# Two up-products of the token-routed experts moved ahead of the output block of the first half's tiles

## The reference

```python
expert_ids = jnp.minimum(clip(token_ids, 0, 12499) // 3125, 3)
for e in range(4):
    g = silu(einsum('bsd,fd->bsf', x, W[e]))
    u = einsum('bsd,fd->bsf', x, W[e])
    y = einsum('bsf,df->bsd', g * u, W[e])
    out = where((expert_ids == e)[..., None], y, out)
x = layernorm(x + out)
```

## Time and profile before

| | |
|---|---|
| median of 3 runs | 702.3 us (701.1 to 705.02) |
| the profiled execution | 701.97 us |
| its span, first to last instruction | 699.9 us |
| TensorE busy | 659.2 us (94%) |
| VectorE busy | 468.1 us (67%) |
| ScalarE, GpSimd busy | 348.6 us, 346.6 us |
| mean granted TensorE clock | 0.990 of full |

### The profile page before, as it was taken

The page is one execution under the profiler, slowest core; times in us unless marked ns, Lnnn a source line. Parts: engine busy times, 40 slices in busy tenths (PEclk is TensorE's granted clock), DMA queues, the critical chain, the costliest instruction groups (busy, mean ns, idle before and its releaser), DMA issues.

```text
span 699.9 us, 12735 instructions
## 1 busy us (share of the span) xinstructions
PE 659.2 (94%) x4598; PEld 511.8 (73%) x4598; DVE 468.1 (67%) x1085; ACT 348.6 (50%) x807; POOL 346.6 (50%) x476
## 2 busy tenths in 40 slices
PE   8989989899999888889999999999999999999994
PEld 6856668857466645557888888887579888888884
DVE  6579878463154999998866867775375556666555
ACT  4655536151514746356877877776352222222224
POOL 5325416341102786555786766766424444455421
PEclk9999999999999999899999999999999999999998
DMA  8000007001003000000000100000202111111001
GB/s 284 1 2 3 1 2 300 1 1 50 0 1 85 2 15 1 2 1 0 2 1 1 70 1 2 1 1 2 68 23 68 46 46 46 46 45 46 1 1 60
DMA packets 10351, 23.31 MB, mean 33 GB/s; under 512 B 2033, under 2 KB 5074, under 8 KB 9906
## 3 DMA queue, kind: packets, MB, share of 16 engines
q1 hardware_dynamic: 10002, 22.24, 9.6%
q10 hardware_dynamic: 288, 0.26, 0.1%
HBM read 21.45 MB, written 1.05 MB: 32 GB/s over the span
## 4 chain that ended last, share of the span: by engine, by line
PE 75%; DVE 16%; ACT 4%; issue 2%; POOL 1%; DMA 1%; POOLq 0%; SPq 0%; DVEq 0%; ACTq 0%
PE psum L454 42%; DVE A L1504 6%; PE psum L1090 4%; PE psum L1101 4%; PE psum L515 4%; PE psum L492 4%; PE psum L859 2%; PE psum L568 2%; PE psum L910 2%; PE psum L610 1%; DVE A L1368 1%; DVE stats L1241 1%; PE psum L574 1%; DVE x_tok L1238 1%; PE psum L584 1%
## 5 line engine op out<-in xcount | busy, mean ns | idle before, releaser
L454 PE MATMUL psum<-parts 128*128 128x256 f32 (+2 forms) x1440 | 244.1, 327 | 2.2 <-DVE C L1540 1.1
L454 PEld LDWEIGHTS psum<-parts 128*128 128x128 f32 (+1 forms) x1440 | 213.8, 190 | 30.3 <-issue 3.3
L2137 POOL TENSOR_SCALAR probs<-probs,row_rec 128x256 f32<-128x256 f32 x128 | 70.2, 561 | 47.3 <-DVE row_rec L1312 44.3
L2051 ACT ACTIVATE A<-psum 128x512 f32<-128x512 f32 x44 | 26.3, 598 | 115.6 <-PE psum L454 115.5
L1733 ACT ACTIVATE probs<-probs,neg_max 128x256 f32<-128x256 f32 x128 | 63.8, 500 | 32.8 <-DVE neg_max L1303 32.8
L1504 DVE TENSOR_TENSOR_SCAN A<-decay,psum 128x256 f32<-128x256 f32 x128 | 75.4, 663 | 4.2 <-PE psum L910 4.2
L1623 DVE TENSOR_TENSOR A<-A,psum 128x512 f32<-128x512 f32 x44 | 30.1, 686 | 70.6 <-ACT A L2051 58.4
L1303 DVE CUSTOM_DVE_ANT_0 probs<-psum,ctxT 128x256 f32<-128x256 f32 x128 | 48.9, 419 | 38.8 <-PE psum L454 36.7
L454 PE MATMUL psum<-parts,A_rounded 128*128 128x256 f32 x372 | 56.2, 289 | 2.4 <-DVE A_rounded L1444 2.4
L454 PEld LDWEIGHTS psum<-parts,A_rounded 128*128 128x128 f32 x372 | 50.1, 196 | 3.7 <-DVE A_rounded L1444 2.8
L1661 DVE TENSOR_TENSOR parts<-A,parts 128x512 fp32r<-128x512 f32 x44 | 48.9, 1111 | 0.8 <-ACT parts L2058 0.7
(11 more groups left out here) (257 smaller groups left out, 1261.7 us busy)
## 6 DMA issues: line engine op xcount, KB each, us to landing
A<-in_experts SPq DMA_DIRECT2D x12, 384.0 KB, 3.1
C<-in_experts SPq DMA_DIRECT2D x10, 384.0 KB, 3.0
A<-in_w_o SPq DMA_DIRECT2D x1, 2048.0 KB, 12.6
x_tok<-in_x_tok SPq DMA_DIRECT2D x1, 1024.0 KB, 7.1
ctxT<-in_ctxT SPq DMA_DIRECT2D x1, 1024.0 KB, 10.5
A<-in_w_uqT SPq DMA_DIRECT2D x1, 768.0 KB, 6.2
out<-x_tok SPq DMA_DIRECT2D x6, 128.0 KB, 1.8
xT<-in_xT SPq DMA_DIRECT2D x2, 256.0 KB, 4.0
```

The lines of the kernel that those rows point to most:

```text
L454: ins = mm(o, left[l], right[r], start=first and n == 0, stop=last and n == 2, skip_group_check=True)
L2137: last = pool.tensor_scalar(pr, pr, row_rec[:, u % RING[n], j:j + 1], 1.0, ALU.mult, ALU.mult)
```

## The change

TensorE issues the up-products 12 and 13 ahead of the output block of the first half's tiles instead of behind it. No other engine's program changes.

```diff
             up_high(1)
             up_low(0)
             up_low(1)
-            for k in range(2, 12):
+            for k in range(2, 14):
                 if k == 4:
                     ln_transposes(0, 1)
                 up(k)
             final(1, range(4), out1)
-            for k in range(12, 16):
+            for k in range(14, 16):
                 if k == 15:
                     ln_transposes(1, 0)
                 up(k)
```

## The result

The changed kernel took 704.64 us in the median (703.44 to 709.21, 20 runs) against 702.4 (700.71 to 708.46, 20 runs) for the kernel before: ratio 1.0032, 95% interval 1.0017 to 1.0047. It is slower by 2.2 us. That is less than the 0.5% (3.5 us) which the forecast took as the least that can be told, but the interval is clear of one. The forecast was 702.7 in a range of 700.7 to 704.8, and no difference.

The account below looks back on a forecast made before the run. TensorE, busy 94% of the span, was taken as the bound, with VectorE setting the pace just ahead of the block. Late start + 0.4, clock - 1.4 and + 1.7 gave + 0.7 on 701.97: 702.7 us, range 700.7 to 704.8.

Parts of the forecast that it names:

- The late start of the block: First half's output block: product 13 waits for VectorE's product 9, so the block starts 0.41 us late (0.2 to 0.6).
- The idle that moves: Ahead of the normalised tokens' transposes: TensorE idles about 2.8 us, transposes stay 4.17 us behind the block, 2.75 us saved worth nothing.
- The rival in which it isn't needed: Ahead of the transposes: tokens ready earlier, so transposes start when product 14 ends; 698.1 us, chance 0.04.
- The clock: Half-clock falls: the one at 125.75 us in the block goes (1.42 us gained), one behind the new idle comes (1.7 lost).
- the idle moves and the fall moves with it: Main case: fall at the block goes, one comes behind the new idle at the transposes; 702.7 us, chance 0.46.
- the slower rival: The fall in the output block stays and another comes behind the new idle; + 2.1 us, 704.1 us, chance 0.12.

Follow-up runs that it names:

- The two fillers: Unused extra matmuls in TensorE's long idle: ten ahead of the transposes in the changed kernel, mean 702.67 us; nine ahead of the block in the kernel before, 701.88 us.

## Why the prediction was right, and what it got wrong

The forecast of no difference held because 2.2 us is below what it took as tellable. The number was less good: the forecast was 0.7 us above the profiled execution, or 0.3 above the median, and the changed kernel is 2.2 above. 704.64 lies 0.16 us inside the upper end of the range, which had been drawn for a rival whose mechanism didn't happen. That the value falls inside is partly luck.

**The late start of the block** was forecast at 0.41 us. Counted from VectorE's product 8, the block starts 126.82 - 122.96 = 3.86 us behind it instead of 3.27: 0.59 us. Product 12 and product 13 each started 0.15 us after VectorE's product had ended (123.63 to 123.78, 125.21 to 125.36) and not 0.06, and each took 1.46 to 1.58 us from start to start, not 1.37. Behind the block's start 0.1 us comes back: 18.36 us to the hidden products in the changed kernel's fourth trace (126.50 to 144.86), 18.49 in the second of before (125.84 to 144.33), both at full clock. So 0.46 us remain, near the forecast and inside its bounds of 0.2 to 0.6.

**The idle that moves** was right: 2.8 us forecast, 2.76 to 2.78 in four traces; the transposes stayed 4.15 us behind the block. That a cover there is worth nothing beyond the tokens' arrival is shown best by three products moved. The rival in which it isn't needed is out.

**The clock** is the term that was mis-sized. I took one fall away ahead of the block (1.42 us) and put one behind it (1.7), as if both kernels had exactly one in each execution: + 0.3 net. Each price was about right: 1.41 us for the block, and behind the new idle 1.1 (19.49 against 18.38), 1.2 (149.13 - 129.55 = 19.58 in the third trace) and 1.6 (in the second, 19.31 - 18.36 up to the hidden products and 7.70 - 7.03 in them). How often was not: the changed kernel spends 3.8 +- 0.6 us more per execution at half clock. At 0.35 us for each that is 1.3 us. With the 0.46 it makes 1.8 of the 2.18 +- 0.28 us between the means, and 0.4 is left. Taken execution by execution, with 0.35 us off for each us at half clock, the changed kernel stays 0.82 +- 0.18 us above the kernel before, where the late start gives 0.46; whether that is noise or a term that nobody named isn't shown. The two fillers size the clock without the slope: filling the idle took 2.31 +- 0.35 us off the changed kernel's mean and 0.92 +- 0.49 off that of the kernel before, so the new idle costs 1.4 +- 0.6 us more than the old one, not 0.3. The step that failed is "the idle moves and the fall moves with it": the longer idle costs more clock than the shorter one, on the mean, and falls elsewhere may be part of it. The value of 704.1 that I gave for the slower rival was nearer to the measured one, but its mechanism (the fall in the block stays) is not what happened: the block took 11.68 us in all four traces of the changed kernel.

**What stays open.** Filling the new idle took away 6.0 +- 0.7 us at half clock, more than one fall of 3.4 us, and no trace shows two behind that idle. So part of the clock's cost lies in falls elsewhere, and no run shows how the idle brings them. In the changed kernel 3 of 4 traces had a fall near 220 us and in the kernel before none of 3, but 4 of the 7 others had one too. Whether the change makes that fall likelier, or the four traces were unlucky, these runs don't settle. That the difference of the first two traces lay mostly there is therefore no proof that the change caused it. The gain of the kernel with one product moved, 0.34 +- 0.40 us in the mean, is also not shown. No version beat the kernel before by more than its interval.

## What to carry to other kernels

Work that is moved into an idle of its engine must not be the cover of another wait: what counts is the next point where that engine meets the others, and here both meetings hang on VectorE. If work has to be moved, split it so that both idles stay short, though a gain in time by this isn't shown here: one product moved leaves 0.8 and 1.4 us with no fall behind either in two traces, two leave 2.8 us in one piece. A fall costs only where TensorE sets the pace: look up how far apart two rows around it are in a trace with it and in one without. Where times differ by less than a fall or two of the clock, count the time at half clock over many executions, not the falls of two traces.

## What the runs showed of the hardware

A fall of the same length has very different prices by place: 3.4 us at half clock cost 1.41 us in the block of 96 matmuls, 1.1 to 1.6 us behind the new idle, 1.6 us near 220 us (19.83 against 18.22 us) and nothing near 258 us, where TensorE had to wait for VectorE's L1504 four times between 255 and 259 us in the changed kernel's first trace.

A matmul that waits for VectorE's semaphore started 0.15 us after the end of VectorE's instruction in the changed kernel, both for product 12 and product 13, against 0.06 us at the block in the kernel before.

Every fall in the body lasted 3.4 us or twice that, and its place against the same idle varied: at 142.1, with the idle still on, or at 143.5, 1.4 us after its end. In the latter case (second trace of the changed kernel) it reached into the hidden products, which then took 7.70 us instead of 7.03:

```profile
142.13 1.30 PE L472 MATMUL psum<-ident,x_tok 128*128 128x128 f32 x8 [2.78 <-DVE x_tok L1248]
143.19 1.76 PE L723 MATMUL psum<-parts 128*128 128x512 f32 x4
144.75 1.05 PE L732 MATMUL psum<-parts 128*128 128x512 f32 x2
145.60 7.70 PE L492 MATMUL psum<-xT,C 128*128 128x512 f32 x16
```

Extra matmuls that compute nothing used can pay: ten of them made the changed kernel 2.3 us faster in the mean, which brought it back to the time of the kernel before (702.67 against 702.80 us), not below it.
